# Second attention's scores as three f32r passes, queries and keys split beforehand, long probabilities turned in two halves

## The reference, cut to what matters

```python
q = (hidden_states @ q_w.T).reshape(b, s, NH, HD).transpose(0, 2, 1, 3)
...
q = q * cos + _rotate_half(q) * sin
k = k * cos + _rotate_half(k) * sin
...
scores = jnp.einsum('bhqd,bhkd->bhqk', q, kf) / jnp.sqrt(jnp.asarray(HD, dt))
scores = jnp.where(causal, scores, jnp.finfo(dt).min)
attn = jax.nn.softmax(scores, axis=-1)
out = jnp.einsum('bhqk,bhkd->bhqd', attn, v)
```

## Time and profile before

| What | Value |
|---|---|
| Three runs, median | 2478.32 us (2474.03 to 2479.27) |
| The profiled execution's own time | 2475.74 us |
| Its span, first to last instruction | 2473.9 us |
| Query stage | about 850 to 1028 us of the span |
| Second attention | about 1044 to 1870 us |
| TensorE, VectorE, ScalarE, GpSimd busy over the span | 89%, 58%, 33%, 18% |
| Granted TensorE clock, mean | 0.965 of 2.4 GHz |

### The profile page before, as it was taken

The page is one execution under the profiler, slowest core; times in us unless marked ns, Lnnn a source line. Parts: engine busy times, 40 slices in busy tenths (PEclk is TensorE's granted clock), DMA queues, the critical chain, the costliest instruction groups (busy, mean ns, idle before and its releaser), DMA issues. The chain is left out here.

```text
span 2473.9 us, 54382 instructions
## 1 busy us (share of the span) xinstructions
PE 2200.2 (89%) x22608; PEld 1548.8 (63%) x22608; DVE 1428.9 (58%) x2081; ACT 826.4 (33%) x1743; POOL 446.3 (18%) x390
## 2 busy tenths in 40 slices
PE   4899969999997999678888888888887997999997
PEld 3677747777776788434444444444445885888886
DVE  4543323333225354388888888888883333767765
ACT  3322122222213200055555656555553211111114
POOL 0111012212220145301111111111111001222221
PEclk9999989999998999889999999999998998999999
DMA  4121153000007533324333433334335541111101
GB/s 150 70 86 36 69 183 109 17 26 26 0 1 261 176 122 120 117 54 109 87 97 82 104 104 85 98 79 109 100 83 189 195 170 47 39 38 38 35 23 68
DMA packets 171250, 222.61 MB, mean 90 GB/s; under 512 B 36545, under 2 KB 108161, under 8 KB 167329
## 3 DMA queue, kind: packets, MB, share of 16 engines
q1 hardware_dynamic: 170176, 219.38, 28.9%
q10 hardware_dynamic: 864, 0.21, 0.0%
HBM read 148.15 MB, written 71.37 MB: 89 GB/s over the span
## 5 line engine op out<-in xcount | busy, mean ns | idle before, releaser
L1469 ACT ACTIVATE a_prob<-ps,a_nmax 128x256 f32<-128x256 f32 (+7 forms) x512 | 377.4, 739 | 367.8 <-DVE a_nmax L1497 233.3
L1579 PE MATMUL ps<-a_kt,a_q 64*128 64x512 f32 (+5 forms) x1536 | 384.1, 542 | 104.7 <-ACT a_prob L1469 83.2
L1497 DVE TENSOR_REDUCE a_nmax<-ps 128x1 f32<-128x1024 f32 (+3 forms) x256 | 256.7, 1003 | 106.8 <-PE ps L1579 106.3
L1579 PEld LDWEIGHTS ps<-a_kt,a_q 64*128 64x128 f32 x1536 | 144.4, 195 | 203.2 <-ACT a_prob L1469 123.6
L1511 DVE STREAM_TRANSPOSE a_pt_long<-a_prob 128x1024 f32<-128x1024 f32 (+3 forms) x256 | 258.0, 1022 | 0.0
L1593 PE MATMUL ps<-a_pt_long,a_v 32*64 32x256 f32 (+3 forms) x7808 | 227.0, 342 | 0.2 <-DVE a_pt_long L1511 0.2
L1593 PEld LDWEIGHTS ps<-a_pt_long,a_v 32*64 32x64 f32 x7808 | 153.2, 131 | 100.7 <-issue 74.9
L1546 POOL TENSOR_TENSOR a_o<-a_left 128x256 f32<-128x256 f32 x128 | 90.4, 728 | 611.3 <-ACT a_left L1479 611.3
L50 PE MATMUL ps<-f_w_hi,f_hT_hi 128*128 128x512 f32 x432 | 168.5, 390 | 3.6 <-POOL f_hT_lo L1890 3.6
L51 PE MATMUL ps<-f_w_lo,f_hT_hi 128*128 128x512 f32 x432 | 168.6, 390 | 0.0
L52 PE MATMUL ps<-f_w_hi,f_hT_lo 128*128 128x512 f32 x432 | 168.1, 389 | 0.0
(11 more groups left out here) (220 smaller groups left out, 4227.7 us busy)
## 6 DMA issues: line engine op xcount, KB each, us to landing
a_q<-scratch_QT SPq DMA_DIRECT2D x512, 64.0 KB, 2.1
scratch_QT<-k_qo SPq DMA_DIRECT2D x64, 256.0 KB, 2.3
a_v<-scratch_V SPq DMA_DIRECT2D x64, 256.0 KB, 4.7
scratch_OT<-a_o SPq DMA_DIRECT2D x32, 512.0 KB, 3.3
o_of<-scratch_OT SPq DMA_DIRECT2D x32, 512.0 KB, 4.4
f_packed<-in_packed SPq DMA_DIRECT2D x11, 768.0 KB, 5.9
a_kt<-scratch_KT SPq DMA_DIRECT2D x128, 64.0 KB, 4.0
f_scale<-in_scale SPq DMA_DIRECT2D x11, 384.0 KB, 6.0
```

What stands on the lines that cost most here:

```text
L1469: last = nc.scalar.activation(prob[:, n % PRING, s].rearrange("p (a w) -> p a w", w=w), SC[n % 2][:, a, 0:w], ACT.Exp, bias=nmax[:, n % 4, ...
L1497: nc.vector.tensor_reduce(nmax[:, n % 4, 0:1], SC[n % 2][:, :, 0:width(0, t)], AX.XY, ALU.max, negate=True).then_inc(maxed, 1)
L1579: last = pe.matmul(sc[:, a, 0:w], q[r, slot, heads[a * hf], :], kt[r, b, keys], start=not masked, stop=True, skip_group_check=True)
```

## The change

The queries are split in the query stage. After GpSimd's sums, ScalarE copies `qo` into a high part (`high`, two instructions of 512 columns a chunk), VectorE subtracts it from `qo` into a low part (`low`, two more, placed behind the next chunk's multiplies), and SyncE stores four pieces a chunk in place of two. The attention loads high and low tiles, eight DMAs a tile in place of four. Keys are loaded into a staging tile; once a unit, in step 12 of the unit before, ScalarE makes the high part and GpSimd the low part. A score is three f32r passes per row half in place of an fp32 matmul. A long turn is two: `FRONT`, the first 16 blocks, in the step two later, and `BACK`, the rest, where the whole turn stood; the first fronts wait only for half of the values of the unit before (`half_valued`). A few semaphores in the first attention are merged.

```diff
@@ projections1
-        q_stored = [sig(f"q_stored{i}", 32 * NCH // 2, credit=True) for i in range(2)]
+        q_high = sig("q_high", 2 * NCH)
+        q_low = sig("q_low", 2 * NCH, credit=True)
+        q_stored = [sig(f"q_stored{i}", 64 * NCH // 2, credit=True) for i in range(2)]
+        q_split = [[w[s][:].rearrange("p k n -> p (k n)").rearrange("p (i n) -> p i n", i=2) for w in (wk, wd)]
+                   for s in range(2)]
...
                 def store_q(g, c):
                     for i in range(2):
-                        sp.wait_ge(q_sum.sem, q_sum.now(g, 2 * c + i + 1))
-                        sp.dma_start(d["QT"][bass.ds(g, 1), i, :, c * CH:(c + 1) * CH].squeeze(0), qo[:, c % 2, i, :]
-                                     ).then_inc(q_stored[c % 2].sem, 16)
+                        sp.wait_ge(q_low.sem, q_low.now(g, 2 * c + i + 1))
+                        for s in range(2):
+                            sp.dma_start(d["QT"][s][bass.ds(g, 1), i, :, c * CH:(c + 1) * CH].squeeze(0),
+                                         q_split[s][c % 2][:, i, :].bitcast(F32)).then_inc(q_stored[c % 2].sem, 16)
...
                             if i == 0:
-                                pool.wait_ge(q_stored[c % 2].sem, q_stored[c % 2].now(g, 32 * (c // 2)))
+                                pool.wait_ge(q_low.sem, q_low.now(g, 2 * c - 2))
...
+                def high(g, c):
+                    act.wait_ge(q_stored[c % 2].sem, q_stored[c % 2].now(g, 64 * (c // 2)))
+                    for i in range(2):
+                        act.wait_ge(q_sum.sem, q_sum.now(g, 2 * c + i + 1))
+                        nc.scalar.activation(q_split[0][c % 2][:, i, :], qo[:, c % 2, i, :], ACT.Copy
+                                             ).then_inc(q_high.sem, 1)
...
+                def low(g, c):
+                    for i in range(2):
+                        dve.wait_ge(q_high.sem, q_high.now(g, 2 * c + i + 1))
+                        nc.vector.tensor_tensor(q_split[1][c % 2][:, i, :], qo[:, c % 2, i, :],
+                                                q_split[0][c % 2][:, i, :].bitcast(F32), ALU.subtract
+                                                ).then_inc(q_low.sem, 1)
+
                 for g in range(NKV):
                     for c in range(NCH):
                         rotate(g, c)
+                        if g or c:
+                            low(*divmod(g * NCH + c - 1, NCH))
                         if c == 1 and g + 1 < NKV:
                             query_weights(g + 1)
+                low(NKV - 1, NCH - 1)
@@ attention1
-TURNS = {5: [0], 6: [1], 7: [2, 3], 8: [4], 9: [5, 6], 10: [7], 11: [8, 9]}
-TURNS.update({i + 2: [i] for i in range(10, USTEPS)})
+FRONT, BACK, WHOLE = range(3)
+TURNS = {i + 2: [(i, FRONT)] for i in range(LONG)}
+for r, back in {5: (0,), 6: (1,), 7: (2, 3), 8: (4,), 9: (5, 6), 10: (7, 8)}.items():
+    TURNS[r] += [(i, BACK) for i in back]
...
+                    for s in range(2):
+                        for a in range(2):
+                            for j in range(2):
+                                r = a * HD1 + j * HD1 // 2
+                                sp.dma_start(q[s][r:r + HD1 // 2, k % QRING, :, :].bitcast(F32),
...
+                def split_kt(u):
+                    act.wait_ge(kt_in, 16 * 8 * (u + 1))
+                    wait(act, scored, USTEPS * (u - 1))
+                    nc.scalar.activation(kt[0][:, u % NB1, :], kt_stage[:], ACT.Copy).then_inc(kt_hi, 1)
...
                     unit, hf, t, heads = place(n)
-                    if n % USTEPS in (0, LONG):
+                    if n % USTEPS == 0 and part == FRONT:
+                        wait(dve, half_valued, unit)
+                    elif n % USTEPS in (0, LONG):
                         wait(dve, valued, 2 * unit + hf - 1)
...
+                def split_kt(u):
+                    pool.wait_ge(kt_hi, u + 1)
+                    nc.gpsimd.tensor_tensor(kt[1][:, u % NB1, :], kt_stage[:], kt[0][:, u % NB1, :].bitcast(F32),
+                                            ALU.subtract).then_inc(kt_lo, 1)
...
-                        last = pe.matmul(sc[:, a, 0:w], q[r, slot, heads[a * hf], :], kt[r, b, keys],
-                                         start=not masked, stop=True, skip_group_check=True)
+                    for i, (x, y) in enumerate(((0, 0), (0, 1), (1, 0))):
+                        for a in range(2):
...
+                            last = pe.matmul(sc[:, a, 0:w], q[x][r, slot, heads[a * hf], :], kt[y][r, b, keys],
+                                             start=i == 0 and not masked, stop=i == 2, skip_group_check=True)
```

More of the change, by code:

```diff
@@ L1389, in attention1, with last_turn @@
             for u, r in at_step(n, TURNS):
[L1390 to L1391 removed]
+                turn_order += [(u * USTEPS + i, part) for i, part in TURNS[r]]
+        turn_number = {turn: i + 1 for i, turn in enumerate(turn_order)}
+        def last_turn(n):
+            return turn_number[n, BACK if n % USTEPS < LONG else WHOLE]
         with nc.Block() as block:
@@ L1524, in _ @@
                     for u, r in at_step(n, TURNS):
-                        for i in TURNS[r]:
-                            turn(u * USTEPS + i)
+                        for i, part in TURNS[r]:
+                            turn(u * USTEPS + i, part)
                     for u, r in at_step(n, (LONG + 2, USTEPS + 2)):
@@ L2039, in transformer @@
     d["KT"] = scratch("KT", [4, P, T])
-    d["QT"] = scratch("QT", [NKV, 2, P, T])
+    d["QT"] = [scratch(f"QT{s}", [NKV, 2, P, T]) for s in range(2)]
     d["V"] = scratch("V", [NKV, NB1, 32, SEQ // 32, HD1])
```

110 lines of the change are left out of this document (63 added, 47 removed).

## The result

The changed kernel takes 2504.9 us (median of 4 runs, 2502.05 to 2507.45), beside 2478.8 for the kernel before on the same chip: ratio 1.0106, 95% interval [1.0084, 1.0128]. The forecast was 2476.5 with a range to 2495: the miss is 28 us, on the slow side.

What follows compares the result with a forecast made beforehand. It took TensorE and VectorE by turns to bound the attention, and the VectorE-GpSimd ring the query stage. Against 2475.7 us, -36 + 28 + 1.9 + 4.6 = -1.5 gave 2474, as a median 2476.5 us; range 2456 to 2495.

Steps and rivals of the forecast that it cites:

- Three passes: Attention scores between the maxima of steps 18 and 2: three f32r passes save TensorE 1.11 us a unit.
- rivals 1 and 5: Attention: 1, narrow f32r passes dear, 2490 us, chance 0.17; 5, weights not hidden in 64 rows, 2590 us, chance 0.02.
- Turns and VectorE's stretches: Attention, per unit: turns in halves save 0.3 us at steps 2 to 4 and 0.85 us in steps 5 to 18.
- the sum for the attention: Attention: 1.11 + 0.30 + 0.85 = 2.26 us saved a unit, 36 us for 16 units.
- The low parts: Query stage: VectorE's subtractions with two SBUF operands delay GpSimd's sums by 0.91 us in 31 chunks, 28 us lost.
- the ring: Query stage: VectorE's multiplies, GpSimd's sums and hand-overs, 5.27 us a chunk, bound it; nothing covers what is added.
- the 7.0 forecast: Query stage: the ring takes 7.0 us in chunk 1, where the weights' subtraction comes too.
- SyncE's four issues a chunk are hidden: Query stage: SyncE's four store issues a chunk, in place of two, add no time.
- Rival 2: Query stage: the SBUF port changes hands between instructions, delaying the second low part; some 10 us more, 2486, chance 0.14.
- Ends: Query stage's end loses 1.9 us to the last split and store, attention's start 4.6 us to more DMA issues.
- What would show it: Trace signs: unit 48.6 us, ring 6.1 to 6.2, value blocks 0.91 behind wide scores, steps 22 and 23 at 0.50.

Runs made afterwards that it cites:

- e3: The kernel before with only the turns put in two halves, scores still fp32 in one pass; ratio 0.9914 to the kernel before.
- e15: The kernel after plus two additional high-by-high passes per row half ahead of the scores of steps 6 to 17, output unchanged; 2480.6 us.
- e6: The kernel after with VectorE's low parts of the queries replaced in place by a memset that reads nothing; 14.6 us less than the kernel after.
- e2: The kernel after with a second buffer for VectorE's products in the query stage, so it multiplies one chunk ahead of GpSimd's sums; 2481.9 us.
- e7: e2 with one additional high-by-high pass per row half in steps 6 to 17 and the attention's last constants issued ahead of the second query tile; 2466 us.
- e12: e7 without the additional pass; scores of steps 6 to 17 are one fp32 matmul of the high parts per row half; 2445.6 us.
- e17: e7 with two additional passes per row half in steps 6 to 14 only, instead of one in steps 6 to 17; 2460.8 us.
- e10: e7 with the additional pass only in steps 15 to 17; 2470.6 us.
- e16: e7 with two additional passes per row half in steps 6 to 15, none in 16 and one in 17; 2452.0 us.

## Why the prediction was wrong

- **Three passes: 1.07 us a unit, at the price of 1.11, but not as forecast.** e3 to the clean unit of the kernel after is 49.93 - 48.86 = 1.07. Halves of the array do run f32r side by side, and weights stay hidden (rivals 1 and 5 out). But the forecast had all of the 1.11 us between the maxima of steps 18 and 2, and there it is 18.28 - 17.79 = 0.49 against the kernel before, 0.61 against e3. A wide score step came out at 1289.60 - 1288.62 = 0.98 us and not 0.91 (before, 1.14; rows below the list). The step of 256 columns takes 0.63 us, not 0.59, and that of 128, where no saving was forecast, 0.56, not 0.50: steps 22 and 23 take 2.05 and 2.04 us against 1.98 and 1.99 in e3, 0.05 to 0.07 dearer each.
- **Turns and VectorE's stretches, 1.15 us a unit: 1.54.** Maxima 2 to 5: 5.70 to 5.40, the 0.30 forecast. Steps 5 to 18: 26.91 to 25.67, 1.24 and not 0.85. By experiment the turns alone (before to e3) give 50.87 - 49.93 = 0.94. All together a clean unit gained 2.01 us against 2.26, so the sum for a clean unit comes within 0.25 us partly by luck: by stretches, one term was 0.62 us too large and one 0.39 too small.
- **The step that failed is the sum for the attention**, "2.26 us a unit, 36 us for 16". It priced each term with TensorE at 2.4 GHz, and no rival spoke of the clock. By shortening TensorE's work where VectorE bounds (which gained little there) the change took the clock away at steps 12 to 14 and 17 to 18, and at 1.2 GHz TensorE is the late one at steps 14 and 18. The falls cost 51.18 - 48.86 = 2.32 us a unit, 35 us over 15, against 6 before. e15 removes them alone: the kernel is 24 us faster, beside a miss of 28, net of its own 0.5 us a unit for the passes.
- **The low parts, 28 us: 24.1.** The place is right, and the cause is shown for the chunks without weights (e6), as is the ring as the way to the end (e2). The pair takes 3.28 us in the mean, not 3.45, and a chunk costs 0.75, not 0.91. The chunks with weights took 7.0 to 7.2 us, the 7.0 forecast. In six of the seven VectorE also waited there for a late load, which the forecast ("SyncE's four issues a chunk are hidden") did not see; it showed once the reads were gone (e6). Rival 2's mechanism is there (2.38 us for two low parts), but not its extra cost.
- **Ends, 6.5 us: 9.1.** From the first query tile's issue to that of the last constant it is 15.89 us (1061.33 to 1077.22), 11.63 before: 4.3, forecast 4.6. From the last pair of sums to the first issue it is 10.21 us, 5.33 before: 4.9, where 1.9 was forecast. Of these, 2.1 are GpSimd's longer pair and the last split, and 2.7 are SyncE's wait between the last result and the first load, 5.6 us now and 2.85 before, which the forecast hadn't counted. No run looks into that wait.
- **"What would show it"** named a unit of 48.6 us, a ring of 6.1 to 6.2, value blocks 0.91 us behind wide scores and 0.50 us for steps 22 and 23. The unit came once in sixteen, at 48.86; the others were 6.03, 0.98 and 0.56.

TensorE in unit 4, the start of a wide score step and of the value blocks behind it:

```profile
1288.62 0.49 PE L1640 MATMUL ps<-a_kt_hi,a_q_hi 64*128 64x512 f32 x1
1289.60 1.23 PE L1654 MATMUL ps<-a_pt_long,a_v 32*64 32x128 f32 x48
```

The hint was there to be read. PEclk in the earlier trace rows is 0.97 for the attention, not 1.00, and 5 of 15 units before were disturbed at steps 12 to 14, by 1.1 to 2.1 us. I took my terms from an undisturbed unit and never asked what kept the others from being one.

## What to carry to other kernels

Before making TensorE's work cheaper in a stretch that another engine bounds, look at the granted clock there and behind it: the time saved may be what holds 2.4 GHz for the stretch that follows. Read several repeats of a unit, not the best one; a few longer ones mark a margin that the change will use up. Work that an idle TensorE can discard is a cheap test of this, and here also the remedy. And measure the parts of a change alone: one part (0.9914) was worth as much as any version of the whole that computes the same.

## What was not expected of the hardware

- At equal or more busy time f32r passes held the clock less well than fp32 matmuls (e7: 11.71 and 7.91 us, 7 of 15 disturbed; e12: 10.94 and 7.19, 1 of 15).
- A unit's outcome isn't set by its instructions: falls came in every unit, in turn, or in a cycle of four, and moving a pass by a few steps changed the pattern (after, e17, e10, e16).
- VectorE writing 128x512 f32 without reading (0.49 us each) leaves GpSimd's sums at 1.27 us; reading two tiles of SBUF makes them 1.64.
